# Sorting stage of a graph network: key rows stored by tile, operations over five tiles, batches of 2, 2 and 1

## The reference

```python
h = jnp.maximum(_layernorm(x), 0.0)
edge_mats = (edge_attr_16 @ W_bond + b_bond).reshape(-1, 32, 32)
for _ in range(4):
    msg = jnp.einsum('eij,ej->ei', edge_mats, h[nbr])      # nbr = dst
    agg = jax.ops.segment_sum(msg, dst, num_segments=n_atoms)  # by src
    h = _gru_cell(agg, h, W_ih, W_hh, b_ih, b_hh)
x = x + h
h = jnp.maximum(_layernorm(x), 0.0)
norm = deg_inv_sqrt[row] * edge_weight * deg_inv_sqrt[col]
x = x + segment_sum(h[row] * norm[:, None], col)
```

## Time and profile before

| | |
|---|---|
| time, median of 3 executions | 30029.33 us (30025.87 to 30030.98) |
| profiled execution | 30022.3 us |
| its span from first to last instruction | 30020.5 us |
| count block | about 46 to 1455 us |
| placing block | about 1505 to 5866 us |
| its scatters on POOL | 1631.2 to 5862.3 us |
| mean granted TensorE clock in the placing | 0.50 |

### The profile page before, as it was taken

One profiled execution on the slowest core, in us unless ns is written; L12 is line 12 of the kernel. 1 busy time (PEld: TensorE's weight loads), 2 busy tenths in 40 slices (PEclk: granted clock), 3 DMA queues, 4 the chain that ended last, 5 costly groups with the idle time before them and its releaser, 6 DMA issues. The chain is left out here.

```text
span 30020.5 us, 295457 instructions
## 1 busy us (share of the span) xinstructions
PE 14803.7 (49%) x72221; PEld 11376.6 (38%) x72222; DVE 10783.8 (36%) x35992; ACT 7681.6 (26%) x24111; POOL 20078.1 (67%) x21002
## 2 busy tenths in 40 slices
PE   3389999744554444444454544445454400000089
PEld 3366666533333333333333333333333300000089
DVE  8789999722222222222222222222222300000044
ACT  9977777611111111111111111111111100000000
POOL 0077777677777677777677777677777677777700
PEclk6655555577777677777677777677777655555555
DMA  3000000111111111111111111111111111111111
GB/s 146 0 14 16 16 16 16 20 28 28 29 28 28 27 28 28 29 28 29 27 28 28 29 28 29 27 28 29 28 28 29 25 46 43 43 43 42 36 36 40
DMA packets 1766515, 932.08 MB, mean 31 GB/s; under 512 B 1175189, under 2 KB 1669316, under 8 KB 1757636
## 3 DMA queue, kind: packets, MB, share of 16 engines
q0 software_dynamic: 671776, 322.48, 7.6%
q1 hardware_dynamic: 523940, 533.80, 6.3%
q10 hardware_dynamic: 570240, 70.85, 1.5%
HBM read 650.58 MB, written 280.42 MB: 31 GB/s over the span
## 5 line engine op out<-in xcount | busy, mean ns | idle before, releaser
L954 POOL DMA_INDIRECT h_rows<-h_table,rec x13824 | 13042.9, 943 | 4331.3 <-issue 4096.8
L1102 PE MATMUL outer<-a_masked,h_by_quarter 128*128 128x136 f32 x27648 | 5123.0, 359 | 8937.9 <-DVE h_by_quarter L995 8937.9
L1102 PEld LDWEIGHTS outer<-a_masked,h_by_quarter 128*128 128x128 f32 x27648 | 4850.1, 260 | 9413.9 <-issue 9413.9
L1148 ACT COPY outer_sums<-outer 128x272 f32<-128x272 f32 x6912 | 2642.0, 385 | 14585.7 <-PE outer L1102 13880.1
L995 DVE TENSOR_TENSOR h_by_quarter<-h_rows,gates 128x2048 f32<-128x2048 f32 x864 | 1976.8, 2288 | 7206.5 <-DMA h_rows<-h_table,rec 7206.5
L1367 POOL DMA_INDIRECT messages_by_bucket<-ms,ix x3456 | 3457.9, 1001 | 1073.5 <-issue 1052.2
L731 POOL DMA_INDIRECT edges_by_node<-row,place x3125 | 2993.6, 958 | 1237.8 <-issue 1237.8
L1078 PE MATMUL msg_psum<-outer_sums,w_bond_blocks 128*128 128x512 f32 x7344 | 3665.6, 647 | 0.0
L988 DVE TENSOR_TENSOR a_masked<-rec,gates 128x2176 f32<-128x2176 f32 x864 | 2090.2, 2420 | 4368.9 <-PE outer L1102 4347.0
L550 PE MATMUL plook<-next_free,ot_f 128*128 128x98 f32 x6250 | 2228.3, 460 | 0.0
L1078 PEld LDWEIGHTS msg_psum<-outer_sums,w_bond_blocks 128*128 128x128 f32 x7344 | 1564.0, 225 | 1562.0 <-issue 1561.7
(11 more groups left out here) (247 smaller groups left out, 20451.0 us busy)
## 6 DMA issues: line engine op xcount, KB each, us to landing
h_rows<-h_table,rec POOLq DMA_INDIRECT x13824, 2.4
rec<-edges_by_node SPq DMA_DIRECT2D x1080, 168.0 KB, 2.3
carry_flags<-carry_flags SPq DMA_DIRECT2D x270, 256.0 KB
chunk_sums<-scan_t ACTq DMA_DIRECT2D x864, 64.0 KB
g_of_rows<-g_of_every_chunk SPq DMA_DIRECT2D x216, 256.0 KB, 3.3
messages_by_bucket<-ms,ix POOLq DMA_INDIRECT x3456, 2.2
mr<-messages_by_bucket SPq DMA_DIRECT2D x202, 264.0 KB, 2.7
messages_by_bucket<-zeros SPq DMA_DIRECT2D x33, 1600.0 KB, 40.4
```

The lines of the kernel that those rows point to most:

```text
L954: pool.indirect_dma_start(out=hb[j][:, u, :], out_offset=None, in_=ht, in_offset=bass.IndirectOffsetOnAxis(ap=rec[j][:, u, W_DST:W_DST + 1 ...
L1102: last = pe.matmul(pt[g % RING][:, at:at + KC], hq[j % 2][:, u, :, :].rearrange("p q d -> p (q d)"), am[j % 2][:, u, :, :].rearrange("p k ...
L1148: act.copy(ts[b][:, :, at:at + w].rearrange("p k (u c) -> p u k c", c=CPT), pt[g % RING][:, 0:GPB * KC].rearrange("p (u k c) -> p u k c", ...
```

## The change

In the count block, the source keys are turned once: DVE casts them to fp32, PE transposes 25 slices of them and 25 of the low keys, ACT copies these out of PSUM (7 and 4 copies, in front of its loop), and SP stores them to DRAM, behind its clearing of the tables, so that each tile's 128 keys lie in a row. In the placing SP loads, for each body, these rows spread over all 128 partitions (`key_row`, fp32, 1.6 MB; `low_key_row`, bf16, 0.8 MB), a body ahead.

With that, `turn`, `psame`, `key_t` and `row_of` go. ACT makes the transposed one-hots `ot_f` from `low_key_row` (one `Abs` and one `Relu` over 640 elements for five tiles), and copies the keys (`take_keys`), from which DVE builds the one-hots of a whole body in three or four operations. The body has five groups of S = 5 tiles. DVE multiplies `nextb` and `plook` by the one-hots over 5x98 elements and sums each with one `tensor_reduce`. `nextb` holds five columns of 98, one for each tile of the group, so PE advances all of them with six matmuls of 490 columns for a group. `nextf` is copied once for a batch (2, 2 and 1 tiles) instead of once a tile; within a batch of 2, the second tile's count of repetitions runs over 256 keys instead of 128. The constants of the comparisons are in PSUM (`pcon`). The pieces of `place_stage` come one in each group, the last at the end of the body. PE uses `pairs_after_first` as well.

```diff
+                    for n in range(NKT):
+                        act.wait_ge(s_turn, n + 1)
+                        act.copy(keys_t[0:IT1, u:u + m, :], pkt[n % 2][0:IT1, 0:m, :]).then_inc(s_turned, 1)
...
+                BATCHES = ((0, 2), (2, 4), (4, S))
...
@@ sync
+                        sp.wait_ge(s_rp, it * NS + NS)
+                        sp.dma_start(key_row[b][:], keys_d[e].unsqueeze(0).broadcast_to([P, EI])).then_inc(s_kr[b], 16)
                         sp.wait_ge(s_row, it + 1)
@@ scalar
+                            for k in range(NB3):
+                                c = (it * NS + s) * NB3 + k
+                                act.wait_ge(s_add, c)
+                                if s == 0 and k == 1:
+                                    take_keys(it + 1, 1 - b)
+                                act.copy(nfs[k][:], nextf[:, 0:HB]).then_inc(s_nf, 1)
+                            transposed(it + 1, 1 - b, i + b, s)
                         act.wait_ge(s_ld[b], i * 48 + 48)
                         act.wait_ge(s_sc[b], i * (16 * J1))
                         act.copy(row[b][:, :, 0:KA], at_[b][:])
@@ vector
+                            dve.tensor_tensor(prod_b[:], bank(nextb), o_bd[:, b * J1 + s * S:b * J1 + s * S + S, :], ALU.mult).then_inc(s_bxr, 1)
...
+                            for j0, j1 in BATCHES:
+                                for j in range(j0, j1):
+                                    u, m = s * S + j, j - j0 + 1
+                                    last = dve.scalar_tensor_tensor(out=junk[j][:, 0:m, :], in0=by_tile[:, u - m + 1:u + 1, :], scalar=key_f[b][:, u:u + 1],
+                                                                    in1=pcon[:, 4 - m:4, :], op0=ALU.is_equal, op1=ALU.mult,
+                                                                    accum_out=rep_[b][:, u:u + 1])
...
+                            dve.tensor_reduce(bpos[b][:, tiles], prod_b[:], AX.X, ALU.add).then_inc(s_bp, 1)
+                            if s < len(builds):
+                                builds[s](it + 1, 1 - b)
+                            dve.wait_ge(s_look, t + 1)
...
+                            dve.tensor_tensor(prod_l[:], bank(plook[(b + s) % 2]), o_hi[b][:, tiles, :], ALU.mult).then_inc(s_lr, 1)
+                            if not first:
+                                place_stage(s, ch, it - 1, 1 - b, i + b - 1)
+                            dve.tensor_reduce(look[b][:, tiles], prod_l[:], AX.X, ALU.add).then_inc(s_lk, 1)
```

More of the change, by code:

```diff
@@ L441, in gnn_program @@
             s_ld = [sem(f"edges_loaded{b}") for b in range(2)]
+            s_kr = [sem(f"key_rows_loaded{b}") for b in range(2)]
+            s_lo = [sem(f"low_key_rows_loaded{b}") for b in range(2)]
             s_row = sem("rows_made")
@@ L488, in gnn_program @@
                 ti = sb("slot_t", [P, J1], I32)
-                ptp = [pb(f"ptp{b}", [P, 8, P], BF16) for b in range(2)]
-                psame = [pb(f"psame{b}", [P, 512]) for b in range(2)]
-                plook = [pb(f"plook{b}", [P, 512]) for b in range(2)]
+                plook = [pb(f"plook{k}", [P, 512]) for k in range(2)]
+                pcon = pb("constants_psum", [P, 4, P])
                 nextf = pb("nextf", [P, 512])
@@ L514, in _ @@
                     pe.matmul(nextf[:, 0:HB], ident_f[:], slots[:], start=True, stop=False, skip_group_check=True)
[L515 to L522, removed]
-                                hold(pe)
[L524 to L539, removed]
-                                      skip_group_check=True).then_inc(s_bx, 1)
[L541 to L551, removed]
@@ L555, in _ @@
+                    pairs_after_first(pe, IT1, body)
                 @block.scalar
@@ new lines, in _, with take_keys @@
+                    for n, key in enumerate((lo_s, hi_s, hi_d)):
+                        last = act.copy(key_v[0][:, n, :], of(key, 0))
+                    last.then_inc(s_kv, 1)
+                    for s in range(NS):
+                        transposed(0, 0, 0, s)
+                    def take_keys(it, b):
+                        for n, key in enumerate((lo_s, hi_s, hi_d)):
+                            last = act.copy(key_v[b][:, n, :], of(key, it))
+                        last.then_inc(s_kv, 1)
@@ new lines, in body @@
+                    def body(it, b, i):
+                        for s in range(NS):
+                            for k in range(NB3):
[5 more added lines that the diff above has]
+                            transposed(it + 1, 1 - b, i + b, s)
@@ L606, in _ @@
                     KP = 18
-                    AHEAD = 3
                     c0 = Chain(dve, s_v3)
@@ L684, in _ @@
                     take_keys(0, 0)
-                    for u in range(AHEAD):
-                        build(0, 0, u)
+                    for n in (1, 2, 3):
+                        builds[n](0, 0)
                     def body(it, b, i, first):
                         ch = Chain(dve, s_v3, (it - 1) * KP + base) if not first else None
-                        for u in range(J1):
-                            t, k = it * J1 + u, ring(b, u)
+                        by_tile = key_row[b][:].rearrange("l (u p) -> l u p", u=J1)
+                        for s in range(NS):
+                            t = it * NS + s
+                            tiles = slice(s * S, (s + 1) * S)
```

258 lines of the change are left out of this document (162 added, 96 removed).

## The result

The changed kernel takes 30,177.3 us (median of 4 runs, 30,172.4 to 30,180.3) against 30,029.7: a ratio of 1.0049, with a 95% interval of 1.0034 to 1.0064. It is slower by about 148 us, where 115 us of gain were forecast. The time lies in the range that was given; the sign is the other one. On one of the chips used further down, executions of one and the same kernel lie at two levels some 40 to 50 us apart, so times are compared there with the kernel before on that chip, and stages between traces.

A forecast was written before the change was run, and what follows sets the result against it. The way through POOL's scatters was taken to bound the placing, ACT the count block. Placing -31 and count -84 made -115 us, 29,915 against the median of 30,029.33; range for 8 in 10: 29,800 to 30,200.

The forecast's parts named there:

- The count block: Count block, bound by ACT: the table load leaves the loop (-86 us), an added cast costs 2; sum -84 us.
- DVE's body: Placing: DVE's products, sums, counts, one-hots and placing operations for one body of 25 tiles sum to 33.5 us.
- T: Placing: time of a body of 25 tiles, stage 94.4 + 122 T; forecast 33.65 us, 33.9 before.
- The loop's edge: Placing: DVE's 2.95 us wait on the loop's first operation, once in two bodies, was taken as gone.
- Rival 3: Placing: the wait at the loop's edge stays, DVE's body 34.9 us; +121 us, whole 30,066; chance 0.12.
- Rival 2: Placing: DVE's counts of repetitions don't overlap, body 37.0 us; +377 us, whole 30,322; chance 0.15.
- PE and ACT: Placing: PE needs 28 us a body and ACT some 14, so neither bounds and both run ahead of DVE.
- POOL: Placing: POOL's own 25 scatters take 31.6 us a body, which lies under the forecast body of 33.65.
- Rival 1: Placing: POOL becomes the bound, body about 31.8 us; -257 us, whole 29,688; chance 0.08.
- The way through the scatters: Placing: from complete place through scatters to DVE's look-ups, two neighbouring bodies take at least 67.3 us; stage -31 us.
- E: Placing: the end of a DVE body; the first group's look-ups were forecast at E + 36.75 us.
- rival 4: Placing: `key_row` load collides with the last scatter, which lands 3.8 us later; +200 us, whole 30,145; chance 0.10.

The follow-up runs named there:

- e4b: The kernel before with one activation ahead of the loop of counts: 29,980.2 us, ratio 0.9971.
- e3: The changed kernel with the five pieces of placing in groups 0, 0, 1, 1, 2 instead of one in each: 29,846.6 us, ratio 0.9940.
- e1: The changed kernel with SP's load of `key_row` issued behind the three loads that wait for the row: 29,944.2 us, ratio 0.9973.
- e7: The changed kernel with each 1.6 MB load of key rows issued as two of 0.8 MB: ratio 0.9659 on one chip, 1.0047 on another.

## Why the prediction was wrong, step by step

- **The count block: right.** -84 was forecast, -86.2 is in the trace, and e4b gives -86.1 by the one load alone. The block's new work, transposing and copying the keys, is hidden in it.
- **DVE's body: right.** 33.5 us was forecast. The short bodies are 32.9; without their waits the long ones are 38.7 - 4.94 = 33.8, on average 33.3; e3, which DVE bounds, has T = 33.2.
- **The loop's edge: right.** DVE stands at most 0.14 us before any of its 625 products of `nextb`, where the earlier trace rows had 2.95 us, and the queue of instructions moved 79 packets instead of 514. Rival 3 falls. That the packets are what the engine had waited for was not tried.
- **The counts side by side: right.** One count is released 0.27 us behind another, one of 256 elements 0.40. Rival 2 falls.
- **PE and ACT: right in that neither bounds.** In the stretch 3000 to 5000 of the changed kernel PE is busy 61% and ACT 34% of the time, at a mean granted clock of 0.70, where PE had 92% at 0.50 in the same stretch before.
- **POOL: right.** It is no bound: its 25 scatters take 31.26 us, and it stands 1.6 us before the next 25 even in the short bodies of 32.9. Rival 1 would have needed DVE under 32.
- **The way through the scatters: this is the step that failed.** Its terms were E - 0.6, + 0.8, + 31.2, **+ 1.2 for the landing**, + 0.8, + 0.25, + 3.1. POOL's start (0.80) and the 25 scatters (31.27) hold. The 1.2 came from a body of the kernel before in which no large transfer stood beside the scatter; it is 4.93 in the changed kernel, 3.7 us more. That is the prediction's own sign of being wrong, ACT's row copy waiting over 3 us longer for the scatters. e1 takes the transfer away and has the 1.2 back, and 233 of the 262 us between forecast and measurement with it.
- **The rest** is 29 us by the medians (e1 took 29,944 where 29,915 was forecast) and 35 by the spans (29,942.5 for 29,907). From the release of ACT's row to DVE's look-up there are 4.43 us (4428.72 to 4433.15) instead of 0.8 + 0.25 + 3.1 = 4.15, and two bodies take 67.9 instead of 67.3: 0.3 a body, 37 us, of which the count block gives 2 back.

The mechanism had been seen: rival 4 says it with place, bytes and price, and gives 30,145 (35.55 a body, 33.5 and 37.6 in turn; measured 32.9 and 38.7). Its price of 3.8 us, from 1.6 MB at 428 GB/s, is what was measured within 0.1. It held one chance in ten. The forecast's own numbers had what was needed to weigh it more. It has the load released 2.6 us before E and the place complete 0.6 before, so the load comes 2.0 us ahead of the place (measured 1.7). The 25th scatter ends 0.8 + 31.2 = 32.0 us after the place ahead was complete, which with bodies of 33.5 is 1.5 us before this one (measured 0.8). So the load is issued 0.5 us before the scatter's instruction ends (measured 0.94). Both times hang on DVE's body, so it was no chance that they fall together: as long as 25 scatters take a little less than a body, they meet again after every short one. The forecast took a price for the landing from a quiet body and put the collision aside as one case among several, instead of laying the issue time of each new transfer beside the end of the wait that the sum rests on.

## What to carry over

A small transfer that somebody waits for (here 128 rows scattered from a tile) is priced with what else is on the queues at that moment; look up when each new large load is released, and issue it just behind the awaited one. Here 3.7 us in every second body outweighed what the other edits gave. The better cure was slack: the same work, with the place completed two groups earlier, made the collision harmless and turned +0.5% into -0.6%. When long and short bodies alternate, read both kinds before you average.

## What the runs showed of the hardware

- A scatter of 128 rows landed 1.2 us after its instruction on quiet queues. With a broadcast load issued 0.8 to 1.1 us before the instruction's end it landed 3.6 us after it (0.8 MB), 5.1 (1.6 MB, and no more with a second 1.6 MB behind) and 5.9 (3.2 MB in packets of 25.6 KB), as medians. Up to 1.2 MB of the load went ahead of the scatter's first packet; then the packets of both went in turn. POOL's instructions in the middle of a place, for whose landing nobody waits, went on at 1.26 us beside the same loads.
- The activation table was loaded inside a loop, 62 times, as long as no activation stood ahead of it; one ahead of it saved 86.1 us in 125 iterations.
- The same kernels can stand in another order on another chip: 1.0047 for the changed kernel with e7's edit on one, 0.9659 on the other, where POOL stood 19.6 us between places. Why is not known.
